# Attention's first tile in halves, learning rates in column groups of TensorE, and a memory stage that starts without the rates' weight

## The chip, the cores and the metric

The program runs on one core of a Trainium2 chip. The number reported is the device time of one execution in microseconds (us). The core has five engines that run in parallel, each through its own list of instructions in order: TensorE (PE, matrix products; PEld is its weight load), VectorE (DVE), ScalarE (ACT), GpSimd (POOL) and SyncE (SP, which here only issues DMAs). They wait for each other by counting semaphores, `wait_ge(sem, n)`.

## The reference

Four stages follow each other, each with a residual sum and a layer norm. X is 4 sequences of 1024 tokens with 256 columns.

```python
# stage 1: gated linear attention, 16 heads of 16
q = _feature_map(q * SCALE); k = _feature_map(k)          # elu(x) + 1
gate = sigmoid(x @ Wg.T + bg)                             # one per token and head
S = g_t * S + k_t * v_t ;  y_t = q_t @ S                  # scan over the 1024 tokens
# stage 2: shared expert and top 2 of 8 routed experts
# stage 3: "memory": gradients of a two-layer silu MLP on (keys, values), one AdamW step, read with the queries
alr = MAX_ALR * sigmoid(x @ Wlr + blr)                    # one rate per token
def loss_fn(ps):
    pred = _lmm(ps, kf)
    return sum(mean((pred - vf) ** 2, axis=-1) * alr)
# stage 4: MLP with ternary weights
```

## The kernel before, in words

The program is a row of blocks: attention, shared expert with routing, routed expert tiles ("ro_"), a small block that only clears semaphores, the memory stage ("m_"), and reading with the last MLP ("q_"). At the end of a block all engines meet.

**Attention** handles the tokens in 32 tiles of 128 (j), four tiles (one of each sequence) to a time step T. An outer loop over n from -5 to 32 is written out on each engine: while tile n is attended, the scores of tile n+1, the projection Q = n+5 and, for T+1, the gates are made. Projections 0 to 3 (queries and keys of T=0) end in four PSUM banks. ACT turns each into relu(-x), relu(x) and exp; `phi` on DVE (for Q < 4, later on POOL) adds the last two. Gates leave ACT as `gT`, are written to DRAM (`gd`, by `gates_out`) and come back by `gates_in` broadcast to all 128 partitions as `gbc` (16 heads by 128 tokens, 1 MB). `decay(j)` is a scan of 2048 columns on DVE over `gbc` that makes the decay matrix `dcy`. `weigh(j)` multiplies the scores, PSUM `bS`, by it, `weigh_k` takes the turned keys. For the first tile the order on DVE is phi(0), phi(1), decay(0), phi(2), phi(3), weigh(0); PE makes scores(0) once all four phi are done.

**The memory stage** works on 8 blocks of 512 tokens (q). It begins with the shared expert on the last 512 tokens (four chunks f: two products on PE, Silu on ACT, product `hs[f]` on DVE, then a product with `Wout_s`), since that was left for this stage. Meanwhile POOL gathers the routed experts' outputs by 8 indirect DMAs a block (`fetch`), DVE adds them and makes the statistics (`combine`, `scales`), ACT normalizes, PE turns X. Then come `keys`, `targets`, `rates`, `first` of block 0. The loop over q on PE is: second(q), grad1(q-1), turn_h0, turn_x(q+1), turn_h1, keys, targets, rates (q+1), back(q), turn_dz2, first(q+1), grad2(q), turn_dz1. `rates` multiplies the tokens by `lr_w`, the weight column Wlr repeated into 128 columns, so that the rate of each token comes out on every partition; ACT applies Sigmoid into `alr`, and DVE's second(q) multiplies by it. `lr_w` is made by DVE after the weights have been loaded, and counts `init` to 6. PE opens the stage with `pe.wait_ge(init, 6)` and two products with zeros `zb` that clear the gradients' banks `gW`.

## Time and profile before

| | us |
|---|---|
| median of 3 runs | 1439.4 |
| lowest, highest run | 1431.15, 1440.06 |
| the profiled execution | 1432.35 |
| its span, first to last instruction | 1430.6 |
| PE busy | 1333.4 (93%) |
| DVE busy | 797.2 (56%) |
| ACT, POOL busy | 577.5 (40%), 303.3 (21%) |

Busy shares are means over stages with different limits: DVE stands at 9 tenths in the first 8 of 40 slices (attention) and at 2 in the routed stage. The attention stage ends near 292 us, the routed tiles run from 458 to 877, the memory stage from 878 to 1193.

### The profile page before, as it was taken

To read this page: it belongs to the slowest core of one execution; us is meant where nothing else is said; L and a number is where in the kernel's file an instruction comes from. 1 tells how busy PE (TensorE), PEld (TensorE's weight loads), DVE (VectorE), ACT (ScalarE), POOL (GpSimd) and SP (SyncE) were. 2 spreads that over 40 slices of the span, in tenths; PEclk is the share of its full clock that TensorE was granted. 3 is DMA by queue.
4 is the path that set the end of the run, shared out by engine and by line. 5 is a ranking of instruction groups with operands and counts; after the bars stand their busy time and mean duration, and the time that the engine had idled before them with its cause. 6 is when DMAs were issued, how large, how long until landed. Compare 5 with 4: busy or idle time off the path is not lost. (4 is left out here: it accounts for less than half of the span.)

```text
span 1430.6 us, 22465 instructions
## 1 busy us (share of the span) xinstructions
PE 1333.4 (93%) x7684; PEld 847.5 (59%) x7685; DVE 797.2 (56%) x1543; ACT 577.5 (40%) x1271; POOL 303.3 (21%) x345
## 2 busy tenths in 40 slices
PE   7999999899998999999999997789999998899995
PEld 4556666655545666666666664345655564577774
DVE  5999999965331222222222221467778656676764
ACT  5577777541101222222222221234444433566665
POOL 2133333314750000000000003522220000244353
PEclk9999999999999999999999998999999999999999
DMA  5665565574220111111111113212110000000001
GB/s 203 207 199 205 206 210 204 198 266 168 99 82 8 37 44 48 47 44 44 44 44 44 48 48 100 78 30 88 30 30 0 1 0 12 1 1 16 30 16 60
DMA packets 76741, 115.83 MB, mean 81 GB/s; under 512 B 10032, under 2 KB 62576, under 8 KB 72560
## 3 DMA queue, kind: packets, MB, share of 16 engines
q1 hardware_dynamic: 70096, 97.89, 20.3%
q0 software_dynamic: 6144, 16.79, 3.6%
q8 instruction: 52, 0.85, 0.2%
q14 instruction: 33, 0.27, 0.1%
q10 hardware_dynamic: 416, 0.03, 0.0%
HBM read 82.86 MB, written 31.82 MB: 80 GB/s over the span
## 5 line engine op out<-in xcount | busy, mean ns | idle before, releaser
L1759 POOL DMA_INDIRECT m_got<-outs,slot x64 | 61.2, 956 | 566.0 <-DMA outs<-XT 453.9
L1164 DVE TENSOR_TENSOR ro_h<-ro_bB,ro_sl 128x512 f32<-128x512 f32 x71 | 49.1, 692 | 217.3 <-PE ro_bB L1113 217.3
L588 DVE TENSOR_TENSOR_SCAN a_dcy<-a_gbc,a_ident 128x2048 f32<-128x2048 f32 x32 | 142.5, 4453 | 6.0 <-DMA a_gbc<-gd 2.2
L2115 POOL TENSOR_TENSOR q_hr<-q_hf,q_hr 128x512 fp32r<-128x512 f32 x64 | 83.9, 1320 | 283.3 <-ACT q_hr L1956 283.3
L1108 PE MATMUL ro_bA<-Win,ro_xT 128*128 x284 | 134.6, 596 | 0.8 <-ACT ro_xT L1135 0.6
L1120 PE MATMUL ro_bO<-Wout,ro_hT 128*128 x568 | 134.3, 379 | 0.9 <-DVE ro_hT L1157 0.9
L1120 PEld LDWEIGHTS ro_bO<-Wout,ro_hT 128*128 128x128 f32 x568 | 107.8, 190 | 45.6 <-issue 34.6
L1113 PE MATMUL ro_bB<-Wsw,ro_xT 128*128 x284 | 133.4, 592 | 0.0
L1144 ACT ACTIVATE XT<-ro_bO 128x256 f32<-128x256 f32 x71 | 27.2, 383 | 204.9 <-PE ro_bO L1120 204.9
L1157 DVE COPY ro_hT<-ro_bH 128x512 f32<-128x512 f32 x71 | 49.1, 691 | 101.2 <-PE ro_bH L1093 101.2
L1113 PEld LDWEIGHTS ro_bB<-Wsw,ro_xT 128*128 128x128 f32 x284 | 54.0, 190 | 67.9 <-issue 67.9
L1881 PE MATMUL q_bO<-W2r,q_hr 128*128 128x256 f32 x512 | 75.8, 293 | 6.8 <-POOL q_hr L2115 6.7
L1139 ACT ACTIVATE ro_sl<-ro_bA 128x512 f32<-128x512 f32 x71 | 42.4, 597 | 96.1 <-PE ro_bA L1108 96.1
L1881 PEld LDWEIGHTS q_bO<-W2r,q_hr 128*128 128x128 f32 x512 | 66.1, 188 | 19.9 <-POOL q_hr L2115 14.2
L597 DVE TENSOR_TENSOR a_A<-a_bS,a_dcy 128x1024 f32<-128x1024 f32 x64 | 75.0, 1212 | 2.3 <-PE a_bS L335 2.3
L1009 POOL DMA_INDIRECT rows<-r_row,r_rix x64 | 63.3, 989 | 61.2 <-DVE r_rix L910 42.1
L676 POOL TENSOR_TENSOR a_qk<-a_eb,a_rb 128x512 f32<-128x512 f32 x28 | 40.0, 1430 | 164.0 <-ACT a_eb L442 164.0
L1871 PE MATMUL q_bH<-q_xr,W1r 128*128 128x512 f32 x256 | 70.7, 404 | 3.6 <-ACT q_hr L1956 3.6
L1108 PEld LDWEIGHTS ro_bA<-Win,ro_xT 128*128 128x128 f32 x284 | 48.3, 190 | 35.5 <-issue 35.2
L1189 PE MATMUL m_ring<-m_h,m_W 128*128 128x512 f32 x128 | 59.9, 612 | 10.0 <-ACT m_alr L1480 6.4
L861 ACT ACTIVATE sh_sl<-sh_bA 128x512 f32<-128x512 f32 x28 | 16.6, 596 | 122.1 <-PE sh_bA L791 67.9
L1955 ACT ACTIVATE q_hf<-q_bH,q_b 128x512 f32<-128x512 f32 x64 | 44.2, 690 | 37.6 <-PE q_bH L1871 36.4
(281 smaller groups left out, 2506.6 us busy)
## 6 DMA issues: line engine op xcount, KB each, us to landing
a_gbc<-gd SPq DMA_DIRECT2D x32, 1024.0 KB, 5.5
rows<-a_zero SPq DMA_DIRECT2D x8, 1152.0 KB, 9.2
XT<-rows SPq DMA_DIRECT2D x71, 128.0 KB, 2.0
outs<-XT SPq DMA_DIRECT2D x71, 128.0 KB, 1.7
a_xt<-in_xTt SPq DMA_DIRECT2D x8, 512.0 KB, 5.8
X<-in_x SPq DMA_DIRECT2D x8, 512.0 KB, 3.9
Win<-in_w_in SPq DMA_DIRECT2D x8, 512.0 KB, 9.8
Wsw<-in_w_sw SPq DMA_DIRECT2D x8, 512.0 KB, 9.8
```

The costliest lines, as they stand in the source:

```text
L588: v.tensor_tensor_scan(dcy[:, :], gbc[j % 2][:, :], ident16[:, :], 0.0, ALU.mult, ALU.add).then_inc(d_done, 1)
L597: v.tensor_tensor(A[j % 2][:, 2 * h:2 * h + 2, :, :, :].rearrange("p r g e t -> p r g (e t)"), bS[:, 2 * h:2 * h + 2, :].rearrange("p r (g ...
L1009: pool.indirect_dma_start(out=mem["rows"], out_offset=bass.IndirectOffsetOnAxis(ap=rix[p][k][:, 0:1], axis=0), in_=row[p][k][:, :], in_off ...
L1108: mm = pe.matmul(bA[:, :], xT[p][:, g, :], w, start=(g == 0), stop=(g == G - 1))
L1113: mm = pe.matmul(bB[:, :], xT[p][:, g, :], w, start=(g == 0), stop=(g == G - 1))
L1120: mm = pe.matmul(bO[:, 0:D], hT[:, j * P:(j + 1) * P], Wout[:, bass.ds(e, 1), j, :].rearrange("p o f -> p (o f)"), start=(j == 0), stop=(j ...
L1157: v.tensor_copy(hT[:, :], bH[:, :]).then_inc(ht_read, 1)
L1189: mm = pe.matmul(banks[o][:, :], W[:, i, col + o * P:col + (o + 1) * P], rhs(i), start=(i == 0), stop=(i == G - 1))
L1759: pool.indirect_dma_start(out=got[q % 2][k][:, t, :], out_offset=None, in_=mem["outs"], in_offset=bass.IndirectOffsetOnAxis(ap=slot[:, k, ...
L1871: mm = pe.matmul(bH[f % 2][:, :], W1r[:, g, f * P:(f + 1) * P], xr[q % 2][:, part, g, :], start=(g == 0 and part == 0), stop=(g == G - 1 a ...
L1881: mm = pe.matmul(bO[k // 2][:, (k % 2) * D:(k % 2 + 1) * D], hr[:, part, f % 4, k * P:(k + 1) * P], W2r[:, f, :], start=(f == 0 and part = ...
L2115: pool.tensor_tensor(hr[:, 1, f % 4, :], hf[f % 2][:, :], hr[:, 0, f % 4, :], ALU.subtract).then_inc(hl_done, 1)
```

## The change

Attention's first tile: `gates_out` and `decays_out` write all 128 partitions in one DMA in place of four; the tokens of T=1 are loaded before that; the broadcast of the first tile's gates and the scan over it are cut in two halves of 8 heads; ACT no longer makes relu(x) for Q = 2 and 3, DVE takes it from PSUM inside `phi`; PE does gates(1), project(4) and turn_k(0) ahead of scores(0).

```diff
+                load_x(1)
                 gates_out(0)
-                gates_in(0)
+                first_gates_in()
                 gates_in(1)
-                load_x(1)
@@ PE
                 for n in range(FIRST, LAST):
                     Q = n + 5
+                    if n == -1:
+                        gates(1)
+                        project(4)
+                        turn_k(0)
+                        scores(0)
+                        values(0)
+                        continue
@@ ACT, project(Q)
-                    act.activation(rb[Q % 2][:, :], projected(Q), ACT.Relu, scale=s).then_inc(qk_read, 1)
+                    if Q != 2 and Q != 3:
+                        act.activation(rb[Q % 2][:, :], projected(Q), ACT.Relu, scale=s).then_inc(qk_read, 1)
@@ DVE
+                        v.scalar_tensor_tensor(out=qk[0][:, 1, Q % 2, :], in0=projected(Q), scalar=0.0, in1=eb[Q % 2][:, :],
+                                               op0=ALU.max, op1=ALU.add).then_inc(phi_done, 1)
+                def first_decay(h):
+                    v.wait_ge(g0_in[h], 16)
+                    v.wait_ge(id_done, 1)
+                    c = slice(h * 8 * P, (h + 1) * 8 * P)
+                    v.tensor_tensor_scan(dcy[:, c], gbc[0][:, c], ident16[:, c], 0.0, ALU.mult, ALU.add).then_inc(d_done if h else d0_done, 1)
                     if Q < 4:
                         phi(Q)
-                    if Q == 1:
-                        decay(0)
+                    if Q == 1 or Q == 3:
+                        first_decay(Q // 2)
```

Memory stage: `lr_w` has 32 columns; four column groups of TensorE each take 128 of the 512 tokens, so the rates come out four partition groups high; they go to DRAM (`ad`, 4 rows of 512 B) and return broadcast as `alr`. PE opens the stage on `init` 2 (ones and zb), and waits for 6 ahead of rates(0). ACT does one small Sigmoid after the last Silu. The block that clears semaphores is gone; POOL clears them inside the routed stage.

```diff
+                def spread_rates(q):
+                    sp.wait_ge(lr_read, q + 1)
+                    sp.dma_start(mem["ad"][q], al4[0:P:32, :]).then_inc(al_out, 16)
+                    sp.wait_ge(al_out, 16 * (q + 1))
+                    if q >= 1:
+                        sp.wait_ge(dp_done, 2 * q)
+                    sp.dma_start(alr[:, :], mem["ad"][q].rearrange("k t -> (k t)").rearrange("(o n) -> o n", o=1).to_broadcast([P, 512])).then_inc(al_in, 16)
@@ PE, rates(q)
-                    for g in range(G):
-                        mm = pe.matmul(b[0][:, :], lr_w[:, g, :], tokens(q)(g), start=(g == 0), stop=(g == G - 1))
+                    for k in range(4):
+                        for g in range(G):
+                            mm = pe.matmul(b[0][32 * k:32 * k + 32, 0:P], lr_w[:, g, :], XT[:, g, q * 512 + k * P:q * 512 + (k + 1) * P],
+                                           start=(g == 0), stop=(g == G - 1))
@@ PE, start of the stage
-                pe.wait_ge(init, 6)
+                pe.wait_ge(init, 2)
                 for k in range(2):
                     pe.matmul(gW[k][:, :], zb[:, 0:P], zb[:, :], start=True, stop=False, skip_group_check=True)
...
                 targets(0)
+                pe.wait_ge(init, 6)
                 rates(0)
@@ ACT
-                    act.activation(alr[:, :], pair(q - 1, LR)[0][:, :], ACT.Sigmoid, bias=blr[:, 0:1]).then_inc(lr_read, 1)
+                    act.activation(al4[:, :], pair(q - 1, LR)[0][:, 0:P], ACT.Sigmoid, bias=blr[:, 0:1]).then_inc(lr_read, 1)
+                act.wait_ge(init, 4)
+                act.activation(junk[:, :], ones[:, 0:1], ACT.Sigmoid)
                 normalize(0)
@@ DVE, second(q)
-                    v.wait_ge(lr_read, q + 1)
+                    v.wait_ge(al_in, 16 * (q + 1))
@@ build
-        build_expert_tiles(nc, mem, "ro_", NI, shared=False)
+        build_expert_tiles(nc, mem, "ro_", NI, shared=False, after={"pool": lambda pool: clear_released(nc, pool)})
-        clear_released(nc)
```

On SP the three first `spread_rates` stand ahead of the loads of the ternary weights `T1` and `T2`, the other five behind them.

TensorE's own order at the first tile of attention, before (`a_bS` scores and projections 0 to 3, `a_bY` gates, `a_bQ` projections from 4, `a_bV` values, `a_bK` turned keys):

```order
3 L267 MATMUL a_bY<-a_xt,a_WgT 32x128 x8
4 L258 MATMUL a_bS<-a_xt,a_Wqk 128x512 x8
5 L335 MATMUL a_bS<-a_qm,a_qk 128x256 x8
6 L267 MATMUL a_bY<-a_xt,a_WgT 32x128 x8
7 L258 MATMUL a_bQ<-a_xt,a_Wqk 128x512 x2
8 L280 MATMUL a_bV<-a_Wv,a_xt 128x256 x2
9 L384 MATMUL a_bK<-ident,a_qk 128x128 x2
10 L335 MATMUL a_bS<-a_qm,a_qk 128x256 x8
```

and in the changed kernel:

```order
3 L272 MATMUL a_bY<-a_xt,a_WgT 32x128 x8
4 L263 MATMUL a_bS<-a_xt,a_Wqk 128x512 x8
5 L272 MATMUL a_bY<-a_xt,a_WgT 32x128 x8
6 L263 MATMUL a_bQ<-a_xt,a_Wqk 128x512 x2
7 L389 MATMUL a_bK<-ident,a_qk 128x128 x2
8 L340 MATMUL a_bS<-a_qm,a_qk 128x256 x8
9 L285 MATMUL a_bV<-a_Wv,a_xt 128x256 x2
10 L340 MATMUL a_bS<-a_qm,a_qk 128x256 x8
```

The gates and the projection of the next time step, and the turned keys, have moved ahead of the first scores.

VectorE at the same place, before (`a_qk` is phi, `a_dcy` the scan, `a_A` weigh, `a_kw` weigh_k):

```order
7 L579 TENSOR_TENSOR a_qk<-a_eb,a_rb 128x512 x2
8 L588 SCALAR_TENSOR_TENSOR a_dcy<-a_gbc,a_ident 128x2048
9 L579 TENSOR_TENSOR a_qk<-a_eb,a_rb 128x512 x2
10 L597 TENSOR_TENSOR a_A<-a_bS,a_dcy 128x1024 x2
11 L605 TENSOR_TENSOR a_kw<-a_bK,a_dcy 128x256
```

and in the changed kernel:

```order
7 L593 TENSOR_TENSOR a_qk<-a_eb,a_rb 128x512 x2
8 L608 SCALAR_TENSOR_TENSOR a_dcy<-a_gbc,a_ident 128x1024
9 L595 SCALAR_TENSOR_TENSOR a_qk<-a_bS,a_eb 128x512 x2
10 L608 SCALAR_TENSOR_TENSOR a_dcy<-a_gbc,a_ident 128x1024
11 L619 TENSOR_TENSOR a_A<-a_bS,a_dcy 128x1024 x2
```

Half of the scan now stands behind phi(3).

## Rows read from the trace of the kernel before

**Rows 1.** Windows: length; busy PE, PEld, DVE, ACT, POOL; granted clock, DMA share, GB/s.

```profile
60.00:100.00 40.00, 37.20 (x560) 23.39 (x552) 39.03 (x35) 28.97 (x82) 12.51 (x20) 1.00 0.63 211
...
1000.00:1100.00 100.00, 98.07 (x390) 61.80 (x388) 75.53 (x170) 42.15 (x76) 15.14 (x16) 1.00 0.08 22
```

**Rows 2.** Timeline, attention's first tile: start, length, engine, line, operation, idle before.

```profile
7.24 1.73 SPq L183 DMA_DIRECT2D gd<-a_gT  x4
...
10.02 0.82 SPq L205 DMA_DIRECT2D a_gbc<-gd  x2
...
11.81 0.69 DVE L579 TENSOR_TENSOR a_qk<-a_eb,a_rb 128x512 f32<-128x512 f32 x1 [1.02 <-ACT a_eb L442]
...
14.66 4.42 DVE L588 TENSOR_TENSOR_SCAN a_dcy<-a_gbc,a_ident 128x2048 f32<-128x2048 f32 x1 [2.16 <-DMA a_gbc<-gd]
...
19.01 1.27 DVE L579 TENSOR_TENSOR a_qk<-a_eb,a_rb 128x512 f32<-128x512 f32 x2
...
20.33 2.09 PE L335 MATMUL a_bS<-a_qm,a_qk 32*128 32x256 f32 x16 [6.76 <-DVE a_qk L579]
...
22.55 2.35 DVE L597 TENSOR_TENSOR a_A<-a_bS,a_dcy 128x1024 f32<-128x1024 f32 x2 [2.28 <-PE a_bS L335]
...
28.06 4.42 DVE L588 TENSOR_TENSOR_SCAN a_dcy<-a_gbc,a_ident 128x2048 f32<-128x2048 f32 x1
```

**Rows 3.** DMA view of 0 to 40 us, 40 slices; an issue line (median to landing).

```profile
GB/s 0 70 193 344 306 318 226 4 17 17 8 246 401 393 459 410 393 382 344 352 257 418 426 356 143 16 0 0 0 0 0 0 0 57 434 418 148 17 20 20
...
gd<-a_gT SPq DMA_DIRECT2D x8, 8.0 KB, 1.4
```

**Rows 4.** Window between the routed and the memory stage, columns as in rows 1.

```profile
876.50:879.00 2.50, 0.00 (x0) 0.00 (x0) 0.46 (x4) 0.14 (x1) 0.00 (x0) 0.93 0.15 52
```

**Rows 5.** Timeline, start of the memory stage.

```profile
873.37 3.63 SPq L1063 DMA_DIRECT2D outs<-XT  x2
...
878.51 0.27 DVE L1673 MEMSET m_zb<- 128x256 uint32 x1
...
879.04 0.98 POOL L1759 DMA_INDIRECT m_got<-outs,slot  x1 [453.93 <-DMA outs<-XT]
...
885.25 1.03 PE L1384 MATMUL m_gW<-m_zb 128*128 128x512 bf16 x2 [9.03 <-DVE m_lr_w L1679]
...
886.08 15.31 PE L1391 MATMUL m_ring<-XT,Ws 128*128 128x512 f32 x32
```

**Rows 6.** Timeline, end of the expert part and the first turn of X.

```profile
897.97 0.60 ACT L1525 ACTIVATE m_dv<-m_ring 128x512 f32<-128x512 f32 x1 [4.53 <-remote]
...
901.54 1.31 DVE L1702 TENSOR_TENSOR m_dz<-m_ring,m_dv 128x512 f32<-128x512 f32 x2 [6.22 <-PE m_ring L1391]
...
910.56 1.91 PE L1292 MATMUL m_ring<-ident,X 128*128 128x128 f32 x8 [0.48 <-issue]
```

**Rows 7.** Timeline, rates(0) on ACT and first(0) on PE.

```profile
925.36 1.26 ACT L1474 ACTIVATE m_vb<-m_ring,m_bias 128x512 f32<-128x512 f32 x2 [6.30 <-remote]
926.65 1.28 ACT L1480 ACT_TABLE_LOAD   x1
...
929.01 5.37 PE L1189 MATMUL m_ring<-m_h,m_W 128*128 128x512 f32 x7 [6.44 <-ACT m_alr L1480]
```

**Rows 8.** Timeline: gates in attention, rates and their use in the memory loop.

```profile
53.37 0.66 PE L267 MATMUL a_bY<-a_xt,a_WgT 128*32 128x128 f32 x16
...
53.83 1.08 PE L354 MATMUL a_bY<-a_A,a_vz 128*32 128x128 f32 x32
...
1045.21 1.88 PE L1311 MATMUL m_ring<-XT,m_lr_w 128*128 128x512 f32 x4
1046.93 3.60 PE L1189 MATMUL m_ring<-m_dz,m_W2T 128*128 128x512 f32 x8
...
954.25 0.69 ACT L1480 ACTIVATE m_alr<-m_ring,m_blr 128x512 f32<-128x512 f32 x1 [0.45 <-PE m_ring L1311]
...
973.18 1.29 DVE L1638 SCALAR_TENSOR_TENSOR m_u<-m_u,m_alr 128x512 f32<-128x512 f32 x2
```

More of the change, by code:

```diff
@@ L181, in gates_out @@
                     sp.wait_ge(gz_done, T + 1)
[L182 to L183 removed]
+                    sp.dma_start(mem["gd"][T].rearrange("b h t -> (b h) t"), gT[T % 2][:, :]).then_inc(gd_out, 16)
                 def decays_out(T):
                     sp.wait_ge(e_done, T)
[L187 to L188 removed]
+                    sp.dma_start(mem["ed"][T].rearrange("b h t -> (b h) t"), ET[T % 2][:, :]).then_inc(ed_out, 16)
                 def decays_in(j):
@@ L201, in gates_in, with first_gates_in @@
                     if j % 4 == 0:
-                        sp.wait_ge(gd_out, 64 * (j // 4 + 1))
+                        sp.wait_ge(gd_out, 16 * (j // 4 + 1))
                     if j >= 2:
                         sp.wait_ge(d_done, j - 1)
-                    sp.dma_start(gbc[j % 2][:, :], mem["gd"][j // 4, j % 4].rearrange("h t -> (h t)").rearrange("(o n) -> o n", o=1).to_broadcast([P, H * P])).then_inc(gb_in[j % 2], 16)
+                    sp.dma_start(gbc[j % 2][:, :], mem["gd"][j // 4, j % 4, 0:H].rearrange("h t -> (h t)").rearrange("(o n) -> o n", o=1).to_broadcast([P, H * P])).then_inc(gb_in[j % 2], 16)
+                def first_gates_in():
+                    sp.wait_ge(gd_out, 16)
+                    for h in range(2):
+                        sp.dma_start(gbc[0][:, h * 8 * P:(h + 1) * 8 * P],
+                                     mem["gd"][0, 0, 8 * h:8 * h + 8].rearrange("h t -> (h t)").rearrange("(o n) -> o n", o=1).to_broadcast([P, 8 * P])).then_inc(g0_in[h], 16)
+                load_x(1)
                 gates_out(0)
-                gates_in(0)
+                first_gates_in()
                 gates_in(1)
-                load_x(1)
                 sp.dma_start(Wo[:, :, :], io["WoT"].rearrange("(g p) n -> p g n", p=P)).then_inc(wo_in, 16)
@@ L439, in project @@
                     act.activation(nb[:, :], projected(Q), ACT.Relu, scale=-s).then_inc(n_done, 1)
-                    act.activation(rb[Q % 2][:, :], projected(Q), ACT.Relu, scale=s).then_inc(qk_read, 1)
+                    if Q != 2 and Q != 3:
+                        act.activation(rb[Q % 2][:, :], projected(Q), ACT.Relu, scale=s).then_inc(qk_read, 1)
                     act.wait_ge(n_done, Q + 1)
-                    act.activation(eb[Q % 2][:, :], nb[:, :], ACT.Exp, scale=-1.0).then_inc(qk_read, 1)
+                    act.activation(eb[Q % 2][:, :], nb[:, :], ACT.Exp, scale=-1.0).then_inc(qk_read, 2 if Q == 2 or Q == 3 else 1)
                 def gates(T):
@@ L446, in gates @@
                     if T >= 2:
-                        act.wait_ge(gd_out, 64 * (T - 1))
+                        act.wait_ge(gd_out, 16 * (T - 1))
                         act.wait_ge(gz_done, T - 1)
@@ L1207, in build_memory @@
         Wlr = sb("Wlr", [P, G])
-        lr_w = sb("lr_w", [P, G, P])
+        lr_w = sb("lr_w", [P, G, 32])
         ones = sb("ones", [P, P])
@@ L1220, in build_memory @@
             sb(k, [P, G, 512]) for k in ("h0", "h1", "vb", "s1", "s2", "sl1", "sl2", "dv1", "dv2", "u", "dz2", "dz1"))
-        alr = sb("alr", [P, 512])
+        alr, al4 = sb("alr", [P, 512]), sb("al4", [P, P])
+        al_out, al_in = sem("al_out"), sem("al_in")
         tok = {k: sb("t_" + k, [P, 4, D]) for k in ("h0", "h1", "dz2", "dz1")}
@@ L1275, in _ @@
                 sp.dma_start(bq[:, :], io["m_bq"]).then_inc(wx_in, 16)
+                def spread_rates(q):
[5 more added lines that the diff above has]
+                    sp.dma_start(alr[:, :], mem["ad"][q].rearrange("k t -> (k t)").rearrange("(o n) -> o n", o=1).to_broadcast([P, 512])).then_inc(al_in, 16)
+                for q in range(3):
+                    spread_rates(q)
                 sp.wait_ge(k_read, 2 * 3)
@@ L1278, in _ @@
                 sp.dma_start(T2[:, :, :], io["t_W2T"].rearrange("(g p) n -> p g n", p=P)).then_inc(tern_in, 16)
+                for q in range(3, NB):
+                    spread_rates(q)
             @block.tensor
@@ L1678, in _ @@
                 for g in range(G):
-                    v.tensor_scalar(lr_w[:, g, :], ones[:, :], Wlr[:, g:g + 1], None, ALU.mult).then_inc(init, 1)
+                    v.tensor_scalar(lr_w[:, g, :], ones[:, 0:32], Wlr[:, g:g + 1], None, ALU.mult).then_inc(init, 1)
                 def sum_weights():
@@ L2137, in rsqrt_group, with clear_released @@
         link(v.scalar_tensor_tensor(out=y, in0=a, scalar=1.5, in1=y, op0=ALU.add, op1=ALU.mult))
-def clear_released(nc):
+def clear_released(nc, pool):
     ids = sorted(nc.released_uncleared_semaphores)
-    with nc.Block() as block:
-        @block.gpsimd
-        def _(pool):
-            start = 0
-            for k in range(1, len(ids) + 1):
-                if k == len(ids) or ids[k] != ids[k - 1] + 1:
-                    pool.sem_clear(range(ids[start], ids[k - 1] + 1))
-                    start = k
+    start = 0
+    for k in range(1, len(ids) + 1):
+        if k == len(ids) or ids[k] != ids[k - 1] + 1:
+            pool.sem_clear(range(ids[start], ids[k - 1] + 1))
+            start = k
 def build(nc, io, out):
```

32 lines of the change are left out of this document (16 added, 16 removed).

## The prediction

> **What bounds the kernel now.** I read the windows by stage first, then the timeline at the two places that the change touches, then the DMA view. In attention's steady state DVE is busy 39.03 of 40 us, PE 37.20; in the memory loop PE is busy 98.07 of 100 us and DVE 75.53 [rows 1]. So in attention time is won where DVE's chain of scans starts earlier, and in the memory loop where PE has less to do. Between the stages the timeline decides.
>
> At attention's first tile [rows 2] the reader is to see a queue: the gates leave at 7.24, the broadcast is issued at 10.02, the scan starts at 14.66 when it has landed, and takes 4.42; two phi stand behind it until 20.28, and only then can PE make the first scores, after 6.76 us idle. From there DVE weighs at 22.55, but the second scan starts at 28.06, since PE still owes gates, projection, values and turned keys. At the memory stage's start [rows 5] PE sits idle 9.03 us until `lr_w` is made, then runs the expert's products.
>
> The sum is made against the profiled execution, 1432.35. It is 7 us below the median of the runs, 1439.4; the lowest run is 1431.15 and the highest 1440.06.
>
> **A: attention's first tile.** The load of T=1 (512 KB) now stands ahead of the gates' write. Its queue ran at 306 to 344 KB/us and had emptied just before 7 us (226, then 4 GB/s) [rows 3], so the load takes some 1.6 us more, until 8.6. The write is issued at 7.24 as before; its landing takes 1.4 us on an empty queue [rows 3]: between 8.6 and 10.4, I take 9.4 (four issues have become one, which gives 1.3 us back). A broadcast of 1 MB took 14.66 - 10.02 = 4.64 us; for half I take 3.3, since the part that grows with bytes is about 2.6 at the 400 GB/s seen from 12 us on. The first half is there at 12.7, just after phi(1) ends at 12.5. Half a scan is 2.2, two phi 1.27 (with PSUM as a source I assume the same): phi(3) ends at 16.2. PE makes turn_k and scores(0) by 17.8, the other half of the scan ends at 18.4, weigh starts at 18.6, not 22.55: 3.9 won. Since gates(1) and project(4) fill PE's hole and turn_k is done, weigh_k and the second scan follow at once: weigh 2.35, weigh_k 0.42, scan at 21.5 in place of 28.06. That is **6.5 us**. Scores(1) follows weigh(0) at 21 and is done long before the second scan ends, so PE does not take it back; DVE is the bound of what follows, and keeps it. Bounds: 3.9, if something on PE or ACT claims the rest, and 7.5, if the write isn't held up by the load.
>
> The four small writes that become one, for later T, are free: SP has slack of most of a tile's time there.
>
> **B: start of the memory stage.** One meeting of all engines goes. SP's last issue ends at 877.00 and zb is ready at 878.78 [rows 5]; I take 0.8 us for the cleared block, between 0 and 1.3. PE then starts at 878.0 instead of 885.25. The clock window after PE's last work shows 0.93 [rows 4], a fall near its end, so PE would restart at about where it fell; I assume 2.4 GHz holds. The 32 products took 15.31 us, the first ones at 1.2 GHz; at 0.43 each (1.72 for four [rows 8]) they take 13.7. The products end 7.2 + 1.6 + 0.4 (the clearing pair too) = 9.2 us earlier, at 892.2. DVE still waits for the weights, until about 885, ahead of its first product, but PE needs that one only before its fourth chunk, some 10 us after its start, 888.8: nothing. POOL's gathers cannot move, they wait for the last `outs` at 879.04 [rows 5], and 8 of them, at 0.98 plus gaps some 10 us, are issued by 889, so combine(0), now due at 893, finds them. What the profile doesn't explain are ACT's late starts: the third chunk's first product ends at 901.2 - 12 x 0.43 = 896.1, its Silu starts at 897.97 [rows 6], 1.7 late, while POOL issues gathers. The whole expert part now lies under them, so I take off 1.7: **7.5 us**. Bounds: 1 (all of it waits until the gathers are out) and 9.7.
>
> **C: rates(0).** ACT loads the Sigmoid table in the path, 1.28 plus 0.25 of gap, now done while it waits for the statistics; Sigmoid over 128 columns instead of 512 saves 0.3: **1.8 us**. ACT's targets start at 925.36 [rows 7]. PE had ended rates(0) 6.44 us before 929.01, at 922.57, and so targets 1.72 earlier, at 920.85: they were held for 4.4 us, and stay so in this sum; if not, 4.4 more and the slow clock of first(0) (5.37 against 3.0 for seven products, 2) are won. So 1.8 to 8.
>
> **D: rates 1 to 7.** Each took 1046.93 - 1045.21 = 1.72 us of PE. The new form is the gates' form in attention: 16 records of 128x32, busy 0.66, the next instruction 0.46 behind the first [rows 8]. I take 0.66: 1.06 x 7 = **7.4 us**, bounds 0.6 and 1.2 each, so 4.2 to 8.8. PE is the bound there with the other engines waiting, so it counts in full; DVE's share of 75.53 would rise to 78. The rates' new way through DRAM lies beside it: from Sigmoid's end at 954.94 to the use at 973.18 there are 18.2 us. No row has a 256 KB broadcast; a 1 MB one takes 4.64 and an 8 KB write 1.4, so the trip takes between 3 and 7 us with issues: hidden, 11 us to spare. For block 0, Sigmoid ends as first(0) starts, 929.0 [rows 7]; its 5.37 us, DVE's part and second(0) with 3.60 (a record of the same form [rows 8]) come before the use, so not before 938, and the trip ends by 936. The ternary loads move behind the third trip, by some 6 us, and are used three blocks later. The three first waits of SP hold nothing else. The Trainium skill ("DMA: Bandwidth & Descriptors", Anatomy of one DMA) gives a fit of 2.0 us plus bytes by 436 KB/us, an estimate of 2.6 us for the 256 KB; the sum would be the same.
>
> **Sum**: 6.5 + 7.5 + 1.8 + 7.4 = 23.2, so 1409 against the profiled execution and 1416 against the median. As the runs before lie in two groups 8 us apart, with profile and lowest run in one, I name **1412**.
>
> **The rivals.**
> 1. *ACT and DVE are held by the gathers.* For: ACT's two late starts [rows 6, 7] both lie under POOL's indirect DMAs; with the expert part wholly under them, `hs` may be ready only when 16 gathers are out, about 899 to 901, as before. B falls to 1: sum 16.7, 1416 to 1423, I name 1419. Against: its first two Silus were on time under the same gathers. Chance 0.2.
> 2. *No late starts at all*: B 9.2, C 8: sum 31, 1401 to 1408. Chance 0.08.
> 3. *Column groups pay for the change of form.* The gates' rows show the next record 0.46 behind the start, but that next one has the same 32-column form; in the memory loop both neighbours have 128. With 0.5 us at each edge rates would take 1.7 and D is 0, 1416 against the profile, 1420 by the runs' middle. Chance 0.06. The Trainium skill ("TensorEngine Tiling (Array Packing)", Key Properties) says that changing the tiling mode drains TensorE, which would act just so; rows 8 show no such edge on the leaving side.
> 4. *Slower: the trip through DRAM becomes the bound.* DVE's second(q) waits for `al_in`, behind it dz2, and behind that PE's back(q). It decides once a trip takes over 18.2 us, and eats the whole gain beyond 18.2 + 23.2/8 = 21.1 us. At 25 us it would be 1409 + 8 x 6.8 = 1463. Against: no DMA in the rows takes a third of that, and that queue is nearly empty (22 GB/s [rows 1]). Chance 0.03.
> 5. *The early token load costs more*, so that the gates land late: phi(2) and phi(3) now stand behind the first half of the scan. A falls to 4, 1414. Chance 0.05.
>
> The forecast keeps 0.58. A measurement can tell about 1% from no change, here 14.4 us, so a time under 1425. The range that holds 8 in 10 takes in rivals 1, 3 and 5 and both groups of runs: 1402 to 1425, of which the forecast's own is 1405 to 1418. Faster by over 1%: 0.58 + 0.08 and most of rivals 1, 3 and 5, together 0.86; within 1%: 0.11; slower 0.03.
>
> **What would show it.** A: the second scan starts at 21 to 22, PE idle before scores(0) under 1 us, and from then every row of attention 6 to 7 us earlier. B: the clearing pair near 878, expert products 13.7 us long, the first turn of X (910.56 before [rows 6]) 6 to 10 us earlier relative to the stage's start. C: no table load between targets and rates. D: the loop's period on PE down by 1.06, with PE still at 98%. Wrong would be a scan that waits for a second `gbc` half, a Silu that starts over 2 us behind its product, or DVE idle ahead of the product with `alr`.

## The result, and the profile after

The changed kernel took 1426.69 us (median of 6 runs, 1419.01 to 1430.33), the kernel before, with further runs, 1436.7 (1431.15 to 1440.61): a ratio of 0.9924, with an interval of 0.9901 to 0.9947. That is 10 us or 0.8% faster, clear of the interval, but less than the 1% above which the prediction counts a gain. Predicted were 1412 and a range from 1402 to 1425. The profiled execution took 1427.48, 4.9 us under the one before; its span fell from 1430.6 to 1425.7.

Windows of the kernel after, columns as in [rows 1]:

```profile
60.00:100.00 40.00, 36.09 (x565) 23.41 (x556) 38.85 (x40) 29.03 (x86) 13.68 (x20) 1.00 0.63 212
1000.00:1100.00 100.00, 95.38 (x425) 60.17 (x424) 76.09 (x170) 41.39 (x77) 15.17 (x16) 1.00 0.10 30
```

In the memory loop PE was busy 98.07 of 100 us and is now busy 95.38, with DVE's share nearly unchanged (75.53 and 76.09). A smaller share alone would only say that PE has less to do; the loop below shows that it also waits where it did not.

The first tile in the timeline of the kernel after, to be read beside [rows 2]:

```profile
7.31 0.33 SPq L183 DMA_DIRECT2D gd<-a_gT  x1
...
10.31 0.80 SPq L209 DMA_DIRECT2D a_gbc<-gd  x2
...
14.93 2.29 DVE L608 TENSOR_TENSOR_SCAN a_dcy<-a_gbc,a_ident 128x1024 f32<-128x1024 f32 x1 [2.35 <-DMA a_gbc<-gd]
...
19.07 2.09 PE L340 MATMUL a_bS<-a_qm,a_qk 32*128 32x256 f32 x16
...
24.15 4.42 DVE L602 TENSOR_TENSOR_SCAN a_dcy<-a_gbc,a_ident 128x2048 f32<-128x2048 f32 x1
```

The broadcast is issued 3.0 us after the write of the gates, half of it still lands 4.6 us after its issue, PE makes the first scores at 1.2 GHz (2.09, against 1.15 in other runs below), and the second scan starts 3.9 us earlier than at 28.06.

The start of the memory stage in the kernel after, to be read beside [rows 5, 6]:

```profile
875.10 0.38 PE L1423 MATMUL m_gW<-m_zb 128*128 128x512 bf16 x1 [2.00 <-DVE m_magic L1717]
...
890.06 7.17 PE L1435 MATMUL m_ring<-Wout_s,m_dz 128*128 128x256 f32 x32 [0.85 <-DVE m_dz L1744]
...
898.17 1.92 PE L1329 MATMUL m_ring<-ident,X 128*128 128x128 f32 x8 [0.93 <-issue]
...
904.79 0.95 POOL L1801 DMA_INDIRECT m_got<-outs,slot  x1 [0.30 <-issue]
909.50 1.29 DVE L1750 TENSOR_TENSOR X<-m_ring,X 128x512 f32<-128x512 f32 x2 [12.53 <-remote]
909.75 1.09 ACT L1500 ACTIVATE XT<-m_ring 128x512 f32<-128x512 f32 x2 [10.16 <-remote]
910.98 2.04 PE L1211 MATMUL m_ring<-XT,m_Wk 128*128 128x512 f32 x2 [10.90 <-ACT XT L1500]
```

PE turned X at 898.17, 12.4 us earlier than in [rows 6]. But DVE's sum with the expert's product, made by 897.2, and ACT's copy of the turned X both start at 909.5 to 909.8, 3.8 to 4.0 us after POOL has finished the last of 24 gathers (905.74). "remote" is what the profile prints where it finds no releaser. Keys(0) gains only 2.8 us (913.74 before). It is PE's signals that are missing: in the same row of gathers ACT began to normalize (897.51) 0.5 us behind DVE's last step for it (896.97), and PE's turn of X followed ACT 0.7 us later.

In the loop, for q = 1 (timeline of the kernel after; PE's products with W2T are back(q)):

```profile
982.00 0.66 PE L1349 MATMUL m_ring<-XT,m_lr_w 128*32 128x128 f32 x16
...
982.59 3.70 PE L1211 MATMUL m_ring<-m_dz,m_W2T 128*128 128x512 f32 x8
...
986.13 1.04 PE L1375 MATMUL m_ring<-ident,m_dz 128*128 128x128 f32 x8
986.33 0.37 ACT L1520 ACTIVATE m_al<-m_ring,m_blr 128x128 f32<-128x128 f32 x1 [2.96 <-remote]
...
989.21 1.29 DVE L1703 TENSOR_TENSOR m_u<-m_ring,m_u 128x512 f32<-128x512 f32 x2 [5.59 <-remote]
...
990.68 1.09 ACT L1538 ACTIVATE m_t_dz<-m_ring 128x512 f32<-128x512 f32 x2 [3.99 <-remote]
...
991.91 1.32 PE L1400 MATMUL m_gW<-m_t_dz,m_t_h 128*128 128x256 f32 x5 [1.31 <-ACT m_t_dz L1538]
```

The rates are as short as predicted: back(q) starts 0.59 behind their start, where it was 1.72 [rows 8]. But their Sigmoid starts 3.7 us after they end, DVE's sum with back(q) 2.9 us after its product, the copy of turned dz2 3.5 us after its turn, and PE then waits. All three are late in q = 1 to 3; in q = 0 the copy of dz2 is, and the first Sigmoid behind it. POOL issues gathers just then; from q = 4 on, with no gathers left, all is on time. The profile gives modelled ends for matmuls, so it cannot tell a late signal of PE from a late end; I call it a late signal. PE's own next instructions are not late.

### The profile page after: what moved, and what is told of

The parts are those of the page before. It is cut to its first block and busy times, and to the rows that moved or that the text cites. A ratio compares the mean times of both kernels' runs of the same rounds, so it can differ in the third digit from the quotient of the medians.

```text
span 1425.7 us, 22628 instructions
## 1 busy us (share of the span) xinstructions
PE 1333.7 (94%) x7779; PEld 846.9 (59%) x7781; DVE 796.8 (56%) x1544; ACT 574.3 (40%) x1270; POOL 298.2 (21%) x345
## 5 line engine op out<-in xcount | busy, mean ns | idle before, releaser
L602 DVE TENSOR_TENSOR_SCAN a_dcy<-a_gbc,a_ident 128x2048 f32<-128x2048 f32 x31 | 138.1, 4455 | 3.9
L698 POOL TENSOR_TENSOR a_qk<-a_eb,a_rb 128x512 f32<-128x512 f32 x28 | 36.6, 1309 | 164.0 <-ACT a_eb L455 164.0
L1400 PE MATMUL m_gW<-m_t_dz,m_t_h 128*128 128x256 f32 x256 | 58.2, 380 | 5.5 <-ACT m_t_dz L1538 5.2
```

Of the source, the lines that this page charges most:

```text
L602: v.tensor_tensor_scan(dcy[:, :], gbc[j % 2][:, :], ident16[:, :], 0.0, ALU.mult, ALU.add).then_inc(d_done, 1)
L1400: mm = pe.matmul(gW[k][:, i * D:(i + 1) * D], tok[left][:, t, i * P:(i + 1) * P], tok[right][:, t, :], start=False, stop=False, skip_group ...
```

## The experiments

The runs were made in six sets. In three (the first comparison, e5 to e8 on chip 6, e9 to e12 on chip 9) the kernel before took 1435 to 1437 us and the traces show late signals; in the others (e1 to e4 on chip 12, e13 to e16 on chip 11, e17 and e18 on chip 8) it took 1419 to 1420, and not one start has the releaser "remote". So each run is compared with the kernel before of its own set. The sets of one kind stand on different chips, so a difference between runs of two sets is weaker than one within a set. "Stage" is the time from POOL's first gather of the memory stage to the first product of the read stage in the profiled execution. It was 314.6 for the kernel before and 315.7 for the changed one in the first comparison.

| run | median | before | ratio (interval) | late signals | stage |
|---|---|---|---|---|---|
| e1_tile | 1415.06 | 1419.01 | 0.997 (0.9956 to 0.9983) | no | 313.0 |
| e2_start | 1407.81 | 1419.01 | 0.9923 (0.9909 to 0.9936) | no | 299.0 |
| e3_rates | 1411.17 | 1419.01 | 0.994 (0.9926 to 0.9953) | no | 303.5 |
| e4_plain | 1393.38 | 1419.01 | 0.9829 (0.9816 to 0.9843) | no | 291.3 |
| e5_whole | 1426.37 | 1436.73 | 0.9922 (0.9898 to 0.9947) | yes | 316.1 |
| e6_tile_start | 1420.47 | 1436.73 | 0.9877 (0.9858 to 0.9895) | start | 312.9 |
| e7_held | 1412.89 | 1436.73 | 0.9819 (0.9799 to 0.984) | fewer | 301.9 |
| e8_load_behind | 1422.97 | 1436.73 | 0.9898 (0.9869 to 0.9927) | yes | 319.4 |
| e9_held_all | 1403.72 | 1435.48 | 0.9782 (0.975 to 0.9813) | m_al only | 296.8 |
| e10_trip | 1423.77 | 1435.48 | 0.992 (0.99 to 0.994) | start | 311.7 |
| e11_groups | 1424.78 | 1435.48 | 0.9928 (0.9905 to 0.9951) | yes | 310.5 |
| e12_plain_again | 1405.22 | 1435.48 | 0.9791 (0.9773 to 0.9809) | none in stage | 292.8 |
| e13_form | 1404.0 | 1419.07 | 0.9888 (0.9872 to 0.9904) | no | 301.3 |
| e14_many | 1401.16 | 1419.07 | 0.9866 (0.9849 to 0.9884) | no | 300.6 |
| e15_held_no_rates | 1403.89 | 1419.07 | 0.9889 (0.9874 to 0.9904) | no | 298.7 |
| e16_before_held | 1418.97 | 1419.07 | 1.0 (0.9991 to 1.0009) | no | 309.2 |
| e17_whole_again | 1395.41 | 1419.64 | 0.9824 (0.9807 to 0.9841) | no | 292.9 |
| e18_many_again | 1402.7 | 1419.64 | 0.9873 (0.9853 to 0.9892) | no | 297.8 |

(e4 and e12 have no gathers; their stage is counted from 0.18 us after the first expert product, where the others have the first gather. e4, e11 and e12 leave a part of the computation out, as their texts say.)

**Is one kind of chip simply faster?** The traces say no. These are the lengths of the stages (from the first product of one to that of the next, the memory stage from its first gather), in us. e16 is the kernel before with the gathers held, which ran as fast as the kernel before (ratio 1.0); e17 is the changed kernel.

| stage | before, late signals | e16, none | changed, late signals | e17, none |
|---|---|---|---|---|
| attention | 293.0 | 293.5 | 290.0 | 290.0 |
| shared expert, POOL writes rows by indirect DMAs | 165.0 | 155.1 | 163.1 | 155.2 |
| routed tiles | 421.1 | 421.1 | 422.4 | 422.2 |
| memory stage, POOL gathers | 314.6 | 309.2 | 315.7 | 292.9 |
| reading and last MLP | 236.9 | 237.5 | 234.5 | 234.9 |

The kinds differ in the two stages in which POOL issues indirect DMAs, and in the others by 0.6 us at most.

**The parts alone.** e1 is attention's part of the diff on the kernel before, e2 the start of the memory stage, e3 the rates:

```diff
e2:
-                pe.wait_ge(init, 6)
+                pe.wait_ge(init, 2)
...
+                act.wait_ge(init, 4)
+                act.activation(junk[:, :], ones[:, 0:1], ACT.Sigmoid)
...
-        clear_released(nc)
```

> The kernel before with attention's part alone (first tile in halves, one write in place of four, the new order on PE); the memory stage is as before. Theory (the first tile wins 3.9 us at the second scan and hands 1 us of it back by the shared stage): shared stage starts about 2.9 us earlier than 292.98, and everything behind it too; time 3 us under the kernel before, ratio 0.998. Rival (what the tile wins is taken back at the clock of the stages behind, so that it is worth nothing): ratio 1.000. Rival (the tile was worth the predicted 6.5 and something of the memory part took it): ratio 0.9955.

> The kernel before with the start of the memory stage alone: no block that only clears semaphores, PE opens the stage on init 2, the small Sigmoid after the last Silu; rates in 128 columns and without the way through DRAM. Theory 1 (signals of PE reach DVE and ACT only when POOL has issued its gathers): expert products start some 11 us earlier than 886.08 and are done 12 earlier, but DVE's sum with the expert's product and ACT's copy of turned X still wait until all 24 gathers are out, near 909 to 910 less the 4 us that the stage starts earlier by; keys(0) gains 3 us only; total gain 2 to 4 us, ratio 0.998. Rival 2 (the late starts came with the column groups and their DMAs, which now are gone): keys(0) starts near 900, gain 10 us or more, ratio 0.993.

> The kernel before with the rates alone in four column groups and their way through DRAM. Each rates takes 0.60 to the next product in place of 1.72. Theory 1 (late signals belong to POOL's gathers, and how many of PE's signals fall under them depends on the phase): either m_t_dz starts 3 to 4 us late in q = 0 to 3 as in the whole change, and the gain is 4 us, ratio 0.997, or none of them is late and the gain is 8 to 9 us, ratio 0.994. Rival 2 (the 16 small products or the two DMAs of each block hold the signals up, whatever POOL does): m_t_dz late in all of q = 0 to 6, gain under 3 us. If none is late here, the phase that the stage's new start gives is what made them late.

Measured: 4.0, 11.2 and 7.8 us, in sum 23.0, and no signal late in any. My theory's figures for e2 (2 to 4 us) were wrong, because late signals were not there at all. In e1 the second scan starts at 22.57 and the routed stage 6.1 us earlier than in e2, whose attention is that of before (442.56 against 448.62). Of that some 3.8 go again in the memory stage (313.0, against 309.2 in e16 on another chip), where keys(0) takes 6.68 in place of 5.24 and second(0) 6.55 in place of 5.37, both partly at 1.2 GHz after a wait.

**Do the parts add?**

> The changed kernel as it is, once more, beside its parts. On one chip its three parts alone won 4.0, 11.2 and 7.8 us, in sum 23.0 (against 1419.0), with no signal of PE late in the memory stage; in the first comparison (another set of runs, 1436.7 before) the whole won 10 us, with signals 3 to 12 us late. Theory 1 (the late signals belong to the chip or the run, not to the change; without them the parts add): 22 to 23 us under the kernel before, ratio 0.984, and no start of ACT or DVE with a releaser outside the trace. Rival 2 (the parts together shift the phase so that signals fall late, on any chip): 10 us, ratio 0.993, m_t_dz late in q = 0 to 3 again.

> The changed kernel once more. The chips so far fell in two kinds: the kernel before takes 1435 to 1437 us, with late signals under the gathers, or 1419 us with none. On a chip of the second kind: the parts won 4.0, 11.2 and 7.8 us there, and if they add, 23 us and 1396, ratio 0.984; if they don't (the rivals of a shift in phase), 0.99 or more. On a chip of the first kind: 10 us, ratio 0.9925, as twice before.

e5 gave 10.4 us with late signals, rival 2's figure; e17 gave 24.2 without, on the same file, and decides for theory 1: whether signals are late belongs to the chip, and without them the parts add. In e5 the late starts stand in the places and nearly with the lengths of the first comparison (XT 10.10, X 12.55, m_t_dz 6.01). The same place in the timeline of e17:

```profile
887.94 0.94 POOL L1801 DMA_INDIRECT m_got<-outs,slot  x1 [0.30 <-issue]
...
888.66 1.28 DVE L1750 TENSOR_TENSOR X<-m_ring,X 128x512 f32<-128x512 f32 x2
...
889.43 1.91 PE L1329 MATMUL m_ring<-ident,X 128*128 128x128 f32 x8 [0.29 <-ACT X L1494]
...
891.38 1.08 ACT L1500 ACTIVATE XT<-m_ring 128x512 f32<-128x512 f32 x2 [0.53 <-PE m_ring L1329]
...
892.61 3.67 PE L1211 MATMUL m_ring<-XT,m_Wk 128*128 128x512 f32 x8 [1.27 <-ACT XT L1500]
```

POOL issues its gathers without a pause here too (32 in one row), and nothing waits for them: DVE's sum starts as soon as DVE is free, keys(0) 3.2 us behind the turn, not 12.8.

**Are POOL's gathers needed for it?** e12 is e4's kernel on a chip with late signals:

```diff
-                            pool.indirect_dma_start(out=got[q % 2][k][:, t, :], out_offset=None, in_=mem["outs"],
-                                                    in_offset=bass.IndirectOffsetOnAxis(ap=slot[:, k, 4 * q + t:4 * q + t + 1], axis=0)).then_inc(came[q % 2][k], 16)
+                            n = (2 * q + k) * 4 + t
+                            sp.dma_start(got[q % 2][k][:, t, :], mem["outs"][n * P:(n + 1) * P, :]).then_inc(came[q % 2][k], 16)
```

> The changed kernel with POOL's 64 gathers replaced by 64 plain loads of the same size and row length from fixed rows of outs, issued by SP; so the routed outputs that are added are not those of the token (that part of the computation is left out). Theory 1 (POOL's issue of gathers makes PE's signals late): no start of ACT or DVE is late in the memory stage, keys(0) near 900 instead of 910.98, loop period of PE 31.5 less in every q; 12 to 16 us under the changed kernel, 1411 to 1415, ratio to the kernel before 0.983. Rival 2 (the gathers' traffic in the DMA engines and the memory does it, whoever issues it) : late starts stay, within 3 us of the changed kernel. Rival 3 (column groups): late starts stay in the loop, gone at the start.

> The changed kernel with plain loads of fixed rows, issued by SP, in place of POOL's 64 gathers (which rows are added is left out), the same kernel that ran 25.6 us under the kernel before on a chip where no signal came late. Theory 1 (the late signals need POOL's gathers): in a session with late signals none is late in the memory stage here, and the gain is 25 to 28 us, ratio 0.981, 15 under the whole's. Rival (the chip is disturbed by something else): late starts in the memory stage remain. The late starts in the shared stage, under POOL's indirect writes, stay in any case.

e4 ran where no signal is late, and won 25.6 us, so it tells only that the loads cost nothing. In e12, with the same bytes in rows of the same length, no start of the memory stage is late, it won 30.3 us, and the stage takes 292.8, as the whole does where signals are not late (292.9). That speaks for POOL's indirect DMAs as the cause, and against their traffic. It is no clean proof: SP issued its first 24 loads in 16.9 us, before the expert's product was done, and those of later blocks behind the rates' way through DRAM, so they did not lie where the gathers lie, and the place alone matters much, as e7 and e9 will show. ACT's waits by releaser in e12 (total, times, longest), all that is left of "remote", in the shared stage under POOL's indirect writes:

```profile
ACT sh_sl L883 <- remote: 19.5, 2, 10.0
```

**Which part brings late signals into the loop?** e6 leaves the rates as before, e10 keeps only their way through DRAM, e11 only the column groups:

```diff
e10, PE, rates:
-                    for k in range(4):
-                        for g in range(G):
-                            mm = pe.matmul(b[0][32 * k:32 * k + 32, 0:P], lr_w[:, g, :], ...
+                    for g in range(G):
+                        mm = pe.matmul(b[0][:, :], lr_w[:, g, :], tokens(q)(g), start=(g == 0), stop=(g == G - 1))
e11, DVE, second(q):
-                    v.wait_ge(al_in, 16 * (q + 1))
+                    v.wait_ge(lr_read, q + 1)
```

> The changed kernel with the rates as before: attention's part and the start of the memory stage, no column groups and no way through DRAM. Theory 1 (parts add): 15 us under the kernel before, ratio 0.9893, 7 to 8 over the whole. Rival 2 (whole has late signals because of the column groups beside the early start): the whole is no faster than this one.

> The changed kernel with rates in 128 columns and two products as before, but the Sigmoid's first partition still goes through DRAM and comes back as a broadcast: the DMAs without the column groups. Measured beside each other, in a session with late signals: the whole 10 us under the kernel before with four m_t_dz 2.5 to 3 us late, the kernel without column groups and trip 16 us under it with none late in the loop. If the trip's DMAs make the signals late: m_t_dz late in q = 0 to 3 as in the whole, ratio 0.997. If it is the column groups: none late in the loop, ratio 0.988 as without both. Without late signals: 0.989.

> The changed kernel with the column groups but without the trip: the rates are computed and the Sigmoid is made, DVE multiplies by a constant 1 (the rates are left out of the gradients). If the column groups make the signals late: m_t_dz late in q = 0 to 3, ratio 0.992 as the whole. If the trip: none late in the loop and the 7 to 8 us of the shorter rates are won, ratio 0.983. Without late signals: 0.984.

ACT's waits for "remote" in e10, then those in e11:

```profile
ACT sh_sl L883 <- remote: 32.4, 3, 19.6
ACT XT L1499 <- remote: 10.1, 1, 10.1
```

```profile
ACT m_t_dz L1532 <- remote: 14.7, 3, 5.4
ACT XT L1496 <- remote: 10.1, 1, 10.1
ACT sh_sl L883 <- remote: 10.0, 1, 10.0
ACT m_al L1514 <- remote: 7.7, 4, 2.9
ACT m_s L1521 <- remote: 3.9, 1, 3.9
```

With two products of 512 columns nothing in the loop is late, with or without the trip (e10, e6); with the column groups it is (e11). The time from back(q) to back(q+1) on PE tells the sizes; it repeats within 0.1 us between profiles of one kind:

| back(q) to back(q+1), q = | 0 | 1 | 2 | 3 | 4 |
|---|---|---|---|---|---|
| before (e6 and e10 within 0.1) | 31.08 | 30.90 | 30.90 | 30.90 | 31.04 |
| e11, groups alone | 31.83 | 31.50 | 31.49 | 31.50 | 30.22 |
| changed kernel, both (e5, e8 within 0.1) | 34.41 | 31.53 | 31.51 | 31.53 | 30.22 |
| e17, changed kernel, no late signals | 29.97 | 29.98 | 29.97 | 29.98 | 30.21 |

Against e17 the groups alone lose 6.4 us in these rows, about what shorter rates win in the whole loop; trip and groups together lose 9.1. In e11 DVE's sum with back(q) is late once, in the whole three times. On chip 6 the whole was 5.9 us slower than e6, which leaves the new rates out: rival 2 of e6. The totals of e10 and e11 (0.992 and 0.9928, against 0.9877 for e6) follow less well, since the late starts in the shared stage differ from run to run, 10.0 to 41.4 us in the profiles of chips 6 and 9; my forecast of 0.988 for e10 failed by as much.

> The changed kernel with rates as two products of 512 tokens on a weight of 32 columns, in one column group (the form of the column groups without their number; PE is busy as long as with 128 columns); the Sigmoid of partition 0 goes through DRAM. Gathers stay where the changed kernel has them. In the runs before: with 16 small products the signals of rates and what follows came 1.5 to 6 us late under the gathers in q = 0 to 3, with two products of 128 columns none did. If the number of short products in a row makes the signal late: none late in the loop, ratio 0.991 as with 128 columns and trip. If the form of 32 columns does: m_al or m_t_dz late in q = 0 to 3, ratio 0.995.

> The changed kernel with rates as eight products of 128 tokens on a weight of 128 columns (their number halfway to the column groups, the form of before); the Sigmoid of partition 0 goes through DRAM. If the number of short products makes the signal late: m_al or m_t_dz 1.5 to 6 us late under the gathers in q = 0 to 3, ratio 0.995. If the form: none late in the loop, ratio 0.991.

> Rates as eight products of 128 tokens on 128 columns (16 records, as many as the column groups have), trip through DRAM. On a chip without late signals: 18 us under the kernel before, as once before, ratio 0.987. On one with late signals: if the number of short products makes them late, m_al or m_t_dz 1.5 to 6 us late in q = 0 to 3 and ratio 0.995; if the form of 32 columns does, none late in the loop and ratio 0.991.

These were to tell the form (a weight of 32 columns) from the number (16 records), but all three ran on chips without late signals, so that stays open. (e14 and e18 are the same kernel, with as many records as the column groups; e14's text, which calls that halfway, is wrong in this.) They show where the gain of the rates comes from: two products on 32 columns take 1.90, sixteen records on 128 columns 1.95, four groups beside each other 0.66. The first gave a stage of 301.3, no less than the old rates (298.7 in e15).

They also show what the change of form costs at its edges. From the start of targets to that of rates PE takes 3.44 with a weight of 128 columns (e16, e14, e18) and 3.53 with one of 32 (e17, e13); from the start of back(q) to the next product 3.43 and 3.54. That is 0.2 us a block, in one column group as in four.

**Where the gathers lie.** e7 and e9 let POOL wait until a place in the loop where PE's signals are not urgent:

```diff
e9, POOL, fetch(q):
                     if q >= 2:
                         pool.wait_ge(add2, q - 1)
+                        pool.wait_ge(xt_read, 2 * (q - 1))
e7, in its place:
+                        if q == 2:
+                            pool.wait_ge(h1_done, 2)
+                        else:
+                            pool.wait_ge(xt_read, 2 * (q - 1))
```

> The changed kernel with POOL's gathers held: those of block 2 until DVE has h1 of block 0, those of block q >= 3 until ACT has copied the turned X of block q-2, so that none is issued while the expert's product is added and X turned, and in the loop they lie under keys, targets and rates. Theory 1, on a chip or in runs where PE's signals come late under the gathers: keys(0) near 900 instead of 911, m_t_dz on time, 8 to 12 us under the whole. Where no signal is late: within 2 us of the whole, since nothing of PE's chain waits for POOL. Rival 2 (late signals have nothing to do with the gathers): late starts where they were.

> The changed kernel with all gathers of block q >= 2 held until ACT has copied the turned X of block q-2 (in the run before only those of q >= 3; those of block 2 waited for h1 of block 0, so that 16 gathers came in one row from 918.7 to 941.6, the Sigmoid of rates(1) and DVE's sum with back(0) started at 944.0, and PE lost 5.5 us idle and 2.2 at the slow clock). Theory 1 (signals of PE come late under gathers, and what it costs is set by which signals these are): on a chip or in a session with late signals, gathers of block 2 lie at 900 to 910, the Sigmoid of rates(0) is late by 2 to 3 us, the gap at first(1) is gone; 4 to 6 us under the run before, ratio to the kernel before 0.979. Without late signals: the whole's gain, ratio 0.984, and nothing of it from the hold. Rival: what made the row of 16 costly was not its place but something in first(1); then no gain over 0.982.

e7 won 23.8 us on chip 6, 13.5 more than the whole beside it (e5), and e9 31.8 on chip 9, where the whole was not run. Timeline of e9:

```profile
893.81 1.92 PE L1329 MATMUL m_ring<-ident,X 128*128 128x128 f32 x8 [0.83 <-issue]
893.99 1.29 DVE L1750 TENSOR_TENSOR X<-m_ring,X 128x512 f32<-128x512 f32 x2 [1.36 <-PE m_ring L1435]
...
895.77 1.08 ACT L1500 ACTIVATE XT<-m_ring 128x512 f32<-128x512 f32 x2 [0.53 <-PE m_ring L1329]
...
897.00 3.67 PE L1211 MATMUL m_ring<-XT,m_Wk 128*128 128x512 f32 x8 [1.27 <-ACT XT L1500]
897.63 0.94 POOL L1802 DMA_INDIRECT m_got<-outs,slot  x1 [6.16 <-ACT XT L1500]
...
904.03 0.66 PE L1349 MATMUL m_ring<-XT,m_lr_w 128*32 128x128 f32 x16
...
907.54 0.37 ACT L1520 ACTIVATE m_al<-m_ring,m_blr 128x128 f32<-128x128 f32 x1 [2.14 <-remote]
```

The gathers of block 2 start behind keys(0) instead of ahead of it. In this stage only the Sigmoid of the rates is late, six times, with waits of 2.1 to 3.7. First(0) waits for it, and starts at 1.2 GHz (5.37 for 3.67); in the loop PE waits for it once, for 0.45. In e7 blocks 2 and 3 came in one row of 16 gathers, from 918.70 to 941.58, and DVE's sum with back(0) started at 944.13:

```profile
944.04 0.37 ACT L1520 ACTIVATE m_al<-m_ring,m_blr 128x128 f32<-128x128 f32 x1 [8.80 <-remote]
944.13 1.29 DVE L1703 TENSOR_TENSOR m_u<-m_ring,m_u 128x512 f32<-128x512 f32 x2 [5.21 <-remote]
...
944.55 5.83 PE L1211 MATMUL m_ring<-m_h,m_W 128*128 128x512 f32 x8 [5.51 <-ACT m_al L1520]
```

> Attention's part and the start of the memory stage with the rates as before, and the gathers held until ACT has copied the turned X of block q-2. The same hold on the whole change gave a ratio of 0.9782. If the rates' column groups are worth their 7 to 8 us once the gathers lie elsewhere: ratio 0.983 here. If the hold alone made that gain and the column groups still cost what they win: 0.978.

> The kernel before with nothing changed but the hold of the gathers (block q >= 2 waits until ACT has copied the turned X of block q-2). Its trace had two late starts at the stage's start (7.5 us at the Silu of the third chunk, 6.3 at targets(0)) and none in the loop. Theory: the second goes or becomes a late Sigmoid, the first lies under the gathers of blocks 0 and 1 and stays: 0 to 4 us, ratio 0.997 to 1.0. Rival: the hold alone is what made 1404, ratio under 0.99.

Both ran without late signals. There the hold is worth nothing (e16 1.0; e15 won 15.2, the sum of e1 and e2, and so gave neither of its two figures), and with the new rates the gain over the kernel before is 24.2 (e17), without them 15.2 (e15): 9.0 for the rates. What the hold does to the kernel before where signals are late was not tried, nor e9 where they are not.

**The early load.** e8 issues the load of T=1 behind the first broadcast:

```diff
-                load_x(1)
                 gates_out(0)
                 first_gates_in()
+                load_x(1)
```

> The changed kernel with the 512 KB load of T=1 issued behind the first gates' broadcast instead of ahead of the gates' write. In the changed kernel the broadcast was issued at 10.3 and its first half landed 4.6 us later, at 14.9, where 12.7 was predicted. Theory A (the load holds the write and its own bytes share the engines with the broadcast): write and first half land 1 to 2 us earlier, but PE's gates(1) and project(4), which stand ahead of turn_k and scores(0), now wait for the load, so the second scan gains at most 1 us: within 1.5 us of the whole. Rival (the landing is 4.6 us whatever stands before it): the first scan starts at 14 to 15 as before and the second one 1 to 3 us later than in the whole, since PE waits for the load.

The broadcast was issued at 8.70 (9.46 in e5) and the scan started at 13.01 (13.86), PE's gates(1) at 15.58 (13.99), when the load had landed, and the second scan at 22.44 (22.38): nothing was gained there, as theory A said. But the load ahead held the write by little: of the 0.76 us by which the broadcast was earlier, 0.61 came from gates that left earlier (7.16 against 7.77). With the load ahead, the time from the write's issue to the broadcast's was 1.6 to 3.4 in fifteen profiles (1.5 here), and what sets it is open. From issue to scan it was 4.3 here, 4.4 in e5, 3.9 to 4.7 in all, so the rival was right that half a broadcast takes this whatever stands ahead of it. The total, 3.4 us under e5, is no difference that six runs of each can show.

## Why the prediction was wrong

The step that failed is B's, that late starts under POOL's gathers cost 1.7 us (the copy of the turned X alone started 9.7 us after the turn had ended; in e17 it starts with its end), and with it D's "it counts in full". On chips where PE's signals are on time the parts won 23.0 and the whole 24.2, where the sum was 23.2; on chips where they come late under the gathers the whole won 10. That the sum fits the first kind so closely is partly luck: A was worth 4.0 in e1 in place of 6.5, and B with C 11.2 in e2 in place of 9.3. By the prediction's steps:

- **A, 6.5:** right in mechanism, too high. The broadcast was issued at 10.31 in place of 9.4, took 4.6 in place of 3.3 (3.9 to 4.7 in all runs, as long as the 4.64 of the whole one), and the scores at 1.2 GHz held weigh for another 0.7. This is rival 5's outcome, but e8 does not put it down to the load. Second scan 3.9 earlier in the first comparison, 4.4 in e17, 5.6 in e1, depending on this landing and on the clock at the first scores (2.09 or 1.15). Its lower bound, 3.9, was met.
- **B, 7.5:** the step that failed. The cleared block gave 0.8 us as taken (874.28 against 878.24 for the stage's first issue, of which 3.1 came from earlier stages), the products took 13.90 for 13.7, and the turn of X was 12.4 earlier. But "I take off 1.7" for late starts under the gathers should have been all of it: keys(0) came 2.8 us earlier, less than the stage's own start. Measured from the stage's first issue, B was worth nothing. Rival 1, at 0.2, had the mechanism (held until the gathers are out) and the price, but at `hs`, which was on time; what was held is the sum with the expert's product and the copy of the turned X, until 24 gathers were out and not 16. [rows 6, 7] showed both late starts. I argued it away by two Silus that were on time. It needed e17 to see that the step itself is worth its price: there keys(0) came 10.15 us earlier than in e16, and only 1.9 of that came from earlier stages.
- **C, 1.8:** no table load lies between targets and rates, and the late targets(0) of [rows 7] went, though 8 gathers lay over it; the Sigmoid of rates(0) came late instead, by a wait of 2.2. From keys(0) to first(0) it was 13.6 in place of 15.3, so 1.7 of the 1.8 were won. The clock had fallen after PE's 10.9 us of waiting, so that keys(0) took 6.16 for 3.67; first(0) was at 2.4 GHz again.
- **D, 7.4:** each rates gave 1.13 where 1.06 was predicted, and the loop's period fell by 0.93 where no signal is late (29.97 in e17 for 30.90 in e16); the 0.2 between are the edges. "It counts in full" failed in q = 0 to 3, where the new form brought late signals with it; no rival had that. From back(0) to back(7) the loop took 217.4 us, more than the 213.9 of before, where it takes 208.3 in e17. The trip through DRAM took some 5 us (in e12 1.6 from the write's issue to the broadcast's, and 3.4 until that landed) and DVE waited for it in no run: rival 4 did not occur. (The 2.6 us in the prediction come from a fit that the Trainium skill, "DMA: Bandwidth & Descriptors", Anatomy of one DMA, gives for DMAs issued by GpSimd; SP issues this one, and 3.4 was measured.) Rival 3 had the right place and a price too high, 0.5 at each edge for 0.1. The Trainium skill ("TensorEngine Tiling (Array Packing)", Key Properties) says that a change of the tiling mode drains TensorE; the 0.09 and 0.11 us at the two edges agree with it.
- **The ends of the range** were made from rival 1's price for the start alone. With the loop's loss and A's it came to 1427, 2 us above the top. Rival 2 (no late starts, 1401 to 1408) could not come out as written: where no signal is late the kernel before is at 1419 to 1420 too, and has no late targets(0) to win back.

The profile of the kernel before had a sign of the size of this: "remote" for 25.4 us of ACT's waits in the shared stage, also under POOL's indirect DMAs, which I did not weigh.

## What to carry to other kernels

Look up every wait for which the profile finds no releaser, and see what POOL issues at that time: in this case PE's signals came late under indirect DMAs, on some chips and not on others, so measure a change on more than one. Put such DMAs where the signals that fall under them are not urgent; a `wait_ge` on POOL was worth 13.5 us on one chip (e7 against e5), more than the whole change won there, and nothing on a chip without late signals (e16). And ask of each instruction that is moved earlier whether it now falls under such a row.

## What the runs showed of the hardware

On chips 6 and 9 and in the first comparison ACT and DVE waited for signals of PE under rows of 8 to 24 gathers of POOL (0.95 us each, 0.30 apart), for up to 12.7 us in the memory stage; the latest start came 12 us after its product had ended. These waits ended between 4.1 us before and 4.1 us after the end of the row. In the memory stage they stood in the same places each time for one kernel, in the shared stage (up to 19.6 us, in e10) they did not. On chips 8, 11 and 12 there was none, even in a row of 32 gathers. The same changed kernel took 1426.37 on chip 6 and 1395.41 on chip 8.

Sixteen records of 128x32 in a row under the gathers were followed by late signals in every profile of a chip of the first kind, four of 128x512 in the loop in none. Why the chips differ, why signals early in a row are on time, and whether the number or the form of the products matters, is open.

Four column groups beside each other do in 0.66 us what takes 1.9 one after the other, and the change from 128 columns to 32 and back costs 0.1 us each way.
